# Two four-head softmax attentions: products of keys by queries and of queries by keys issued together, in half steps

## What is computed

```python
def _L3_attn_ref(x, Q, K, VO):
    q = jnp.einsum('btd,hrd->bhtr', x, Q)
    k = jnp.einsum('bud,hrd->bhur', x, K)
    scores = jnp.einsum('bhtr,bhur->bhtu', q, k) / sqrt(d)
    attn = jax.nn.softmax(scores, axis=-1)
    ctx = jnp.einsum('bhtu,bud->bhtd', attn, x)
    return jnp.einsum('bhtd,hde->bte', ctx, VO)

def _L3_ffn_ref(x, ln1_w, ln2_w, wq, wk, wv, wo, router_w, w1, w2, w3):
    h = _rmsnorm(x, ln1_w)
    ...
    scores = jnp.einsum('bhtd,bhsd->bhts', q, k) / jnp.sqrt(jnp.float32(HD))
    scores = jnp.where(causal[None, None], scores, jnp.float32(-1e+30))
    att = jax.nn.softmax(scores, axis=-1)
    y = jnp.einsum('bhts,bhsd->bhtd', att, v).transpose(0, 2, 1, 3).reshape(Bx, Tx, Cx)
    x = x + y @ wo.T
```

## Time and profile before

| | us |
|---|---|
| runs (three) | 1031.77, 1028.7, 1040.98 |
| median | 1031.77 |
| span of the profiled execution | 1033.0 |
| PE busy in it | 920.6 (89%) |
| DVE busy | 645.0 (62%) |
| ACT busy | 367.8 (36%) |
| POOL busy | 226.8 (22%) |

### The profile page before, as it was taken

One profiled execution on the slowest core, in us unless ns is written; L12 is line 12 of the kernel. 1 busy time (PEld: TensorE's weight loads), 2 busy tenths in 40 slices (PEclk: granted clock), 3 DMA queues, 4 the chain that ended last, 5 costly groups with the idle time before them and its releaser, 6 DMA issues. The chain is left out here.

```text
span 1033.0 us, 17166 instructions
## 1 busy us (share of the span) xinstructions
PE 920.6 (89%) x6700; PEld 464.5 (45%) x6700; DVE 645.0 (62%) x1728; ACT 367.8 (36%) x644; POOL 226.8 (22%) x289
## 2 busy tenths in 40 slices
PE   1898788889999888999798899999999899989998
PEld 0588566652323346753474333333333444443333
DVE  4978555667765368985547555455553655577665
ACT  0113532334543343225415324444444032342222
POOL 2700022215335123420330310121223402200000
PEclk9989898999999999999957989999999987999999
DMA  9300300000000001000000000000000000000000
GB/s 309 86 1 2 100 2 1 2 2 1 1 1 1 1 1 43 2 1 1 1 1 2 0 1 1 1 1 2 1 1 1 1 1 1 2 1 1 6 6 11
DMA packets 11476, 15.40 MB, mean 15 GB/s; under 512 B 8268, under 2 KB 9324, under 8 KB 10398
## 3 DMA queue, kind: packets, MB, share of 16 engines
q1 hardware_dynamic: 9976, 13.20, 4.1%
q10 hardware_dynamic: 1418, 1.09, 0.4%
HBM read 13.76 MB, written 0.52 MB: 14 GB/s over the span
## 5 line engine op out<-in xcount | busy, mean ns | idle before, releaser
L633 DVE TENSOR_REDUCE mx<-PS 128x2 f32<-128x1024 f32 (+3 forms) x104 | 109.6, 1096 | 98.0 <-PE PS L440 93.9
L593 ACT ACTIVATE arena<-PS 128x1024 f32<-128x1024 f32 (+3 forms) x104 | 91.0, 924 | 129.8 <-PE PS L470 129.8
L1231 DVE TENSOR_TENSOR arena<-arena,PS 128x512 f32<-128x512 f32 (+1 forms) x144 | 97.1, 685 | 45.2 <-ACT arena L1206 40.5
L1132 PE MATMUL PS<-XT,late 64*128 64x512 f32 (+1 forms) x288 | 101.6, 647 | 4.8 <-DVE L L1874 2.0
L485 PE MATMUL PS<-arena 128*64 128x512 f32 (+3 forms) x416 | 101.4, 578 | 0.5 <-DVE arena L694 0.4
L465 PE MATMUL PS<-arena 32*128 32x512 f32 (+4 forms) x416 | 78.4, 625 | 10.2 <-ACT arena L570 7.4
L1206 ACT ACTIVATE arena<-PS,f_b_sb 128x512 f32<-128x512 f32 x96 | 61.9, 686 | 63.6 <-PE PS L1132 62.2
L1164 PE MATMUL PS<-arena,late 128*64 128x512 f32 (+1 forms) x288 | 81.6, 617 | 1.0 <-DVE arena L1231 0.9
L440 PE MATMUL PS<-arena 32*128 32x512 f32 (+4 forms) x416 | 69.3, 609 | 4.2 <-ACT arena L566 1.6
L1132 PEld LDWEIGHTS PS<-XT,late 64*128 64x128 f32 (+1 forms) x288 | 28.5, 184 | 56.4 <-ACT arena L1206 41.5
L1206 ACT ACTIVATE arena<-PS 114x512 f32<-114x512 f32 x48 | 27.4, 596 | 67.6 <-PE PS L1134 66.9
(11 more groups left out here) (427 smaller groups left out, 1675.2 us busy)
## 6 DMA issues: line engine op xcount, KB each, us to landing
arena<-in_rel SPq DMA_DIRECT2D x4, 1024.0 KB, 12.0
late<-in_edges SPq DMA_DIRECT2D x2, 1024.0 KB, 11.1
late<-in_w_f_w SPq DMA_DIRECT2D x3, 342.0 KB
arena<-in_adj SPq DMA_DIRECT2D x1, 1024.0 KB, 6.8
late<-in_w_f_w SPq DMA_DIRECT2D x2, 512.0 KB, 4.1
Cc<-in_consts SPq DMA_DIRECT2D x1, 916.0 KB
arena<-in_ids ACTq DMA_DIRECT2D x1, 800.0 KB
late<-in_w_f_w SPq DMA_DIRECT2D x4, 128.0 KB, 3.5
```

The costliest lines, as they stand in the source:

```text
L593: nc.scalar.activation(PT[:, s % 2, p, :, queries(c)], PS[:, a:a + 2, queries(c)], ACT.Exp, scale=scale).then_inc(exp_done.sem, 1)
L633: v.reduce_max(mx[:, g % 2, c, 2 * p:2 * p + 2], PS[:, a:a + 2, keys(c)], axis=AX.X).then_inc(max_done.sem, 1)
L1132: ins = nc.tensor.matmul(PS[0:rows, up_bank(n), :], w1(i)[r], XT2[r, b * S:(b + 1) * S], start=True, stop=True)
L1231: nc.vector.tensor_tensor(HG[0:rows, n % 4, :], ha, PS[0:rows, gate_bank(n), :], ALU.mult).then_inc(gated_done.sem, 1)
```

## The change

Nothing of the arithmetic changes, and the count of instructions on each engine is the same. In the two four-head attentions a step becomes two half steps. `opposite(s, p)` issues the column products of pair p of step s, then the row products of the other pair of step s+5, then the subtraction for pair p, then (masked) the masks of the other pair. A step is `opposite(s, 0)`, the turned maxima (c = 3) or the projection (c = 2), `mix(s-1, 0)`, `opposite(s, 1)`, the turned input (c = 0), `mix(s-1, 1)`, the output products (c = 1). The list `units` follows this order, so each unit's bank and the unit that it waits for change too. ACT's and DVE's orders follow: exponential of pair 0, copies of turned maxima or projection, exponential of pair 1; on DVE the maxima of one pair at a time, each in front of the zeroing of the pair of column products issued with it. The two-head attention keeps its order. Functions that nothing called are removed.

```diff
         for s, (g, c) in enumerate(steps):
-            units += [("B", s, p) for p in range(NPAIR)]
+            units += [("B", s, 0)]
+            if s + ahead < U:
+                units += [("A", s + ahead, p) for p in range(1, NPAIR)]
             if s == 0 and weights is not None:
                 units += [("W", 0, 0)]
+            if c == 3 and g + 1 < G and NPAIR == 2:
+                units += [("T", g + 1, 0)]
             if c == 2 and g + 2 < G:
                 units += [("P", g + 2, k) for k in range(PU)]
+            units += [("B", s, p) for p in range(1, NPAIR)]
             if s + ahead < U:
-                units += [("A", s + ahead, p) for p in range(NPAIR)]
+                units += [("A", s + ahead, 0)]
...
+                def opposite(s, p):
+                    r = s + ahead if NPAIR == 2 and s + ahead < U else None
+                    column_products(s, p)
+                    if r is not None:
+                        row_products(r, 1 - p)
+                    less_maxima(s, p)
+                    if causal and r is not None:
+                        row_masks(r, 1 - p)
...
                 for s in range(U + 1):
-                    if s < U:
-                        cols(s)
+                    if s == U:
+                        for p in range(NPAIR):
+                            mix(s - 1, p)
+                        break
+                    g, c = steps[s]
+                    opposite(s, 0)
                     if s == 0 and weights is not None:
                         weight_products()
+                    if c == 3 and g + 1 < G and NPAIR == 2:
+                        maxima(g + 1)
+                    if c == 2 and g + 2 < G:
+                        proj(g + 2)
                     if s >= 1:
                         mix(s - 1, 0)
-                    if s == U:
-                        if NPAIR == 2:
-                            mix(s - 1, 1)
-                        break
-                    g, c = steps[s]
-                    if c == 2 and g + 2 < G:
-                        proj(g + 2)
-                    if s + ahead < U:
+                    if NPAIR == 2:
+                        opposite(s, 1)
+                    elif s + ahead < U:
                         rows(s + ahead)
...
                 for s, (g, c) in enumerate(steps):
-                    if causal:
-                        for p in range(NPAIR):
+                    for p in range(NPAIR):
+                        if NPAIR == 2 and s + ahead < U:
+                            maximum(s + ahead, 1 - p)
+                        if causal:
                             x = PT[:, s % 2, p, :, c * P:(c + 1) * P]
                             eng.wait_ge(exp_done.sem, at(exp_done, s * NPAIR + p))
                             v.scalar_tensor_tensor(out=x, in0=x, scalar=3.0e38, in1=bc(causal[1], 1, 2), op0=ALU.min, op1=ALU.mult).then_inc(later_zeroed.sem, 1)
-                    if rope and c == 2 and g + 2 < G:
-                        turned_pairs(g + 2)
+                        if p == 0 and rope and c == 2 and g + 2 < G:
+                            turned_pairs(g + 2)
```

More of the change, by code:

```diff
@@ L6 @@
-from contextlib import ExitStack, contextmanager, nullcontext
+from contextlib import ExitStack, nullcontext
 import numpy as np
@@ L38, in __init__ @@
         self.count = 0
[L41 to L53, removed]
 def bc(ap, axis, n):
@@ L177, in flat @@
         return t[:].rearrange("p a b -> p (a b)")
[L180 to L199, removed]
@@ L588, in _, with exponentials @@
                     qk(g)
+                def exponentials(s, p):
+                    c = steps[s][1]
+                    a = bank(("B", s, p))
+                    eng.wait_ge(cols_done.sem, at(cols_done, s * NPAIR + p))
+                    nc.scalar.activation(PT[:, s % 2, p, :, queries(c)], PS[:, a:a + 2, queries(c)], ACT.Exp, scale=scale).then_inc(exp_done.sem, 1)
                 for s, (g, c) in enumerate(steps):
-                    for p in range(NPAIR):
-                        a = bank(("B", s, p))
-                        eng.wait_ge(cols_done.sem, at(cols_done, s * NPAIR + p))
-                        nc.scalar.activation(PT[:, s % 2, p, :, queries(c)], PS[:, a:a + 2, queries(c)], ACT.Exp, scale=scale).then_inc(exp_done.sem, 1)
+                    exponentials(s, 0)
                     if s == 0 and weights is not None:
@@ L626, in turned_pairs, with maximum @@
                         v.tensor_tensor(RS[:, k, :], PS[:, a + 1, :], rope[1], ALU.mult).then_inc(roped.sem, 1)
+                def maximum(s, p):
+                    g, c = steps[s]
+                    a = bank(("A", s, p))
+                    eng.wait_ge(rows_done.sem, at(rows_done, row_place(s, p)))
+                    v.reduce_max(mx[:, g % 2, c, 2 * p:2 * p + 2], PS[:, a:a + 2, keys(c)], axis=AX.X).then_inc(max_done.sem, 1)
                 def maxima(s):
                     g, c = steps[s]
-                    for p in range(NPAIR):
-                        a = bank(("A", s, p))
-                        eng.wait_ge(rows_done.sem, at(rows_done, s * NPAIR + p))
-                        v.reduce_max(mx[:, g % 2, c, 2 * p:2 * p + 2], PS[:, a:a + 2, keys(c)], axis=AX.X).then_inc(max_done.sem, 1)
+                    if not swapped(s):
+                        for p in range(NPAIR):
+                            maximum(s, p)
                     if c == TB - 1:
@@ L1034, in linear_attention @@
             signal.count += k
-    def weight_products(pairs, dst, split):
-        with stage(pe=1, act=1) as (block, tallies):
-            @block.tensor
-            def _(eng):
-                pe, _, _, _ = tallies()
-                for n, (l, r) in enumerate(pairs):
-                    ins = nc.tensor.matmul(PS[0:D, 0, n * D:(n + 1) * D], l, r, start=True, stop=True)
-                ins.then_inc(pe.up(), 1)
-            @block.scalar
-            def _(eng):
-                pe, act, _, _ = tallies()
-                eng.wait_ge(tensor_done.sem, pe.at(1))
-                nc.scalar.copy(dst[:, 0:len(pairs) * D], PS[0:D, 0, 0:len(pairs) * D]).then_inc(act.up(), 1)
     pickh = sb("pickh", [P, 16], BF16)
```

195 lines of the change are left out of this document (52 added, 143 removed).

## The result

| | before | after |
|---|---|---|
| runs of both on the same chip (twenty each), median | 1034.65 us | 1047.9 us |
| lowest to highest | 1028.27 to 1041.66 | 1041.24 to 1068.88 |
| ratio, 95% interval | | 1.0117 (1.0083 to 1.015) |
| span of the profiled execution | 1033.0 | 1048.8 |
| mean granted clock in it | 0.938 | 0.929 |

The changed kernel is slower by 1.2%, some 12 us, and the forecast was no change at 1032, with 1022 to 1041 around it.

A forecast was written before the change was run, and what follows sets the result against it. TensorE was taken as the bound in the plain attention, busy 175.8 of 181.2 us. Plain -1.1 and masked +2.5 sum to +1.4 on 1033.0; forecast median 1032, no change, range 1022 to 1041 for 8 times in 10.

The forecast's parts named there:

- -5.3: Plain attention, five middle groups: gain of 1.06 each, from the turned maxima's 0.68 wait and late second pairs.
- -1.5: Plain attention, first group: a gain taken as 1.5 us, between 0 and 4, since waits for the first maxima stay.
- +5.7: Plain attention, last five steps: pairs alone lose 7.1 us, less two late second pairs and one wait of 0.68.
- the rival of 1100: Both attentions: row products don't start beside the other pair's column products, some +70 us, 1100; chance 0.02.
- the faster rival: Exponential frees its bank earlier, all halves 2.28 (3.3 us); masked attention keeps 2.4 GHz (5.8 us); 1023; chance 0.2.
- 2.44: Plain attention: length in us of every other half step, its row products waiting 0.36 for the previous half's exponential.
- No wait, with 0.2 to spare: Plain attention, turned maxima: split ready 3.5 us after the half's start at c = 2, TensorE asks at 3.7.
- The mask portions: Masked attention: masks in two portions cost 0.21 us each, +1.0 over eleven steps, +3.6 at the drain rule's bound.
- The waits at c = 3: Masked attention, two groups: 0.6 for the second rotary product's bank, 1.95 at the turned maxima; 2.6 against 1.8, +1.6.
- if the clock does what it does now: Condition on the masked attention's +2.5 us, the sum of +1.0 masks, +1.6 waits, -2.7 late pairs and +2.6 tail.
- 5.8 for 20.5: Masked attention, price of the clock: 20.5 us at the lower level cost 5.8 us, between 0 and 10.3.
- The slower rival: Masked attention: clock falls more often, 41 us at the lower level costing 5.8 more, tail another 4; 1042; chance 0.2.

The follow-up runs named there:

- filled: Kernel before with half steps in the masked attention alone, plus matmuls nobody reads in its waits at c = 3; ratio 1.0049, median 1038.21 us.
- after, unchanged copy: The changed kernel executed once more with nothing changed, for a second trace of its clock; measured 1059.92 us.

## Why the prediction was wrong, point by point

**The plain attention was right in sum, with two errors in it that offset.** Forecast -1.1, made of -5.3, -1.5 and +5.7; measured at equal clock -2.1, made of -5.7, -2.1 and +5.8. A tail step of lone pairs, forecast at 4.57, in the changed kernel:

```profile
779.44 1.13 PE L336 MATMUL PS<-arena 32*128 32x512 f32 x4
...
784.01 1.13 PE L336 MATMUL PS<-arena 32*128 32x512 f32 x4
```

784.01 - 779.44 = 4.57. Row products do run beside the other pair's column products, which disposes of the rival of 1100. A half step in all engines that matter:

```profile
646.03 0.70 PE L336 MATMUL PS<-arena 32*128 32x512 f32 x2
...
646.07 0.70 PE L304 MATMUL PS<-arena 32*128 32x512 f32 x2
...
647.00 0.38 PE L343 MATMUL PS<-arena,minus 32*128 32x512 bf16 x2
...
647.31 1.08 PE L367 MATMUL PS<-arena 128*64 128x512 f32 x4
647.42 1.02 ACT L477 ACTIVATE arena<-PS 128x1024 f32<-128x1024 f32 x1 [1.18 <-PE PS L343]
...
648.32 0.70 PE L336 MATMUL PS<-arena 32*128 32x512 f32 x2
...
648.49 0.70 PE L304 MATMUL PS<-arena 32*128 32x512 f32 x2
```

Here one term was mis-sized. The exponential starts 647.42 - 646.03 = 1.39 behind its column products, not 1.57 as with four heads, and ends at 648.44. Row products start at 648.49, which is 2.46 after the half's start and 0.17 into the next, where I had 2.64 and 0.36. At 0.17 they end inside the column chain, so all halves are 2.28, as the faster rival had it for this part, and the "2.44" didn't come. That gives back 3 x 0.16 a group, 2.4 in the five middle ones. The other error goes the other way: for the split I had "No wait, with 0.2 to spare". In two of the five middle groups there is one, at 711.87 and 757.19:

```profile
711.87 0.38 PE L326 MATMUL PS<-identh,arena 128*128 128x128 bf16 x4 [0.61 <-DVE arena L553]
```

Together these take 1.2 us. So the nearness of the sum is in part luck.

**The masked attention's work was right too.** Forecast +2.5. At 2.4 GHz throughout the half-step order takes 80.1 (filled); that of before takes 78.1 with 3.4 us at the lower level and 80.0 with 10.2, so an estimated 77.1 with none, by the line through both: +3.0. Of this the tail, forecast at +2.6, is +3.2 (80.1 with lone pairs, 76.9 with joined ones, neither with time at the lower level), and all other terms together are -0.2, forecast at -0.1. The mask portions, forecast at 0.21:

```profile
846.66 0.29 PE L312 MATMUL PS<-causalh,identh 128*128 128x128 bf16 x2
...
846.88 0.87 PE L367 MATMUL PS<-arena 128*64 128x384 f32 x4
```

0.22 to the next row. Two masks take 0.22 and four take 0.33, so some 0.11 of a portion doesn't shrink with the masks. The rule on draining in the Trainium skill (TensorEngine Tiling, Key Properties), weighed in the forecast, can have cost at most that here; at its bound of 0.33 the term would have been +3.6.

The waits at c = 3, for which I had 0.6 and 1.95:

```profile
848.34 0.49 PE L336 MATMUL PS<-arena 32*128 32x128 f32 x4 [0.59 <-DVE arena L524]
...
849.68 0.38 PE L304 MATMUL PS<-arena 32*128 32x128 f32 x2 [0.85 <-POOL arena L632]
...
851.08 0.38 PE L326 MATMUL PS<-identh,arena 128*128 128x128 bf16 x4 [0.69 <-DVE arena L553]
```

Their sum is 2.13 (2.6 forecast), in three portions: row products wait for the keys that POOL finishes, a wait that I hadn't counted apart, and that takes most of what I had put at the turned maxima. At the end of the third group the wait is 1.49, as forecast (1.5):

```profile
904.51 0.38 PE L326 MATMUL PS<-identh,arena 128*128 128x128 bf16 x4 [1.49 <-DVE arena L553]
```

**The step that failed** is the clause behind that sum: "if the clock does what it does now". I gave it 0.55 and its opposite 0.2, while the same text said that idle time at c = 3 grows. Two things were wrong in it. First, "now" was one profile: 20.5 us at the lower level. Later profiles of the same order have 3.4, 10.2 and, with the masked attention left as before in the plain half-step kernel, 10.2 again; the half-step order has 23.9, 27.3 and 62.5. Second, the price. From 0 to 23.9, 27.3 and 62.5 us at the lower level the half-step stretch goes from 80.1 to 90.6, 90.8 and 106.4, about 0.42 us for each us, where I took "5.8 for 20.5", 0.28. For the order of before that was near: its loops of 78.1, 80.0, 80.0 and 83.4 us, with 3.4, 10.2, 10.2 and 20.5, rise by 0.31. The half-step order pays more for the same time at the lower level.

One of my signs of being wrong was a clock of the masked stretch that moves by more than 0.05. The first pair of profiles (0.88 and 0.87) doesn't show it; the later ones lie further apart (0.94 and 0.98 with the old order, 0.85 and 0.71 with half steps).

Together: three profiles of the half-step order have a mean of 96.0 us for the masked loop and four of the old order 80.3, which is more than the 12 us measured over many executions; the longest, 106.4, is from a single long execution, and without it the difference is 10. Of this +3.0 is work and waiting, and the rest is the clock's.

**The slower rival** had the mechanism and came near with its price, 1032 + 10 = 1042; the median of before was 2.9 higher in the larger sample. But its condition was at the wrong place. It was to decide where the idle time at the turned maxima exceeds 1.1. In the first two groups that is 0.69, and still the clock fell: the fall at 852.62 came behind three waits of 0.59, 0.85 and 0.69, which lie between 847.75 and 851.08. In the third group it is 1.49, and there the clock fell in one profile of the half-step order (after, unchanged copy) and not in the other two. Nor does the clock fall much oftener, as the rival had it. In four profiles with the old order in the masked attention it falls at seven of the eight ends of a first or second group, behind waits of 0.48 and 0.64, and stays down for 3.4 to 13.7 us, 6.3 on average; in three with half steps it falls at all six and stays down for 10.2 to 17.1, 13.7 on average. What grew is above all the time that it stays down. Nor is the tail a cause by itself, as I had it: with lone pairs and filled waits it stays at 2.4 GHz; what lone pairs seem to do is keep the clock down once it has fallen at the tail's start (37.5 us, in both profiles where it fell there). In three profiles with joined pairs it fell there too, and was up again after 3.4 us each time. No run isolates this.

Shown by experiment: the loss is in the masked attention alone; over half of it goes when the waits are filled with unread work, and in the masked stretch lone pairs cost 3.2 us beside that. With both mended the whole is under before, though a part of that gain lies outside the stretch. Not shown: how little waiting would do, and why work issued in the same order has 88.7 to 136.5 us at the lower level ahead of the attentions. I didn't try the fillers in the old order.

## What to carry to other kernels

When a change leaves a busy TensorE with more or other short waits, price the clock as a term of its own, from several profiles of the same order, and not as something that stays as it is. Work in which only some of the row groups are busy should be kept short: with both pairs together a step of the plain tail is done in 3.15 instead of 4.57 us. And keep it away from a place where the clock may fall, as far as the few profiles here go. And before a wait is moved, ask what else ends within it: one that is released by the copy may be covering one for the maxima.

## What the runs showed of the hardware that I had not expected

- TensorE stayed at the lower level for 37.5 us while it was busy for 36.99 of them, with lone pairs of 32-row products, output products and mixes (a second profile: 37.15 of 37.50); with both pairs together it was up again after 3.4 us in the same part of the program, in three profiles.
- Short waits between groups of matmuls are enough for the clock to fall. At waits of 0.59, 0.85 and up to 0.69 us, close together, it fell each time, eight times in four profiles, in the second wait at the earliest; at 0.48 and 0.64 in seven places of eight. At a single wait it fell not always: at 1.28 once of two times, at 1.48 to 1.50 three times of five. The Trainium skill (TensorE: Matmul & The Clock Gate, A second HAM failure mode: psum-queue depth-cycling) describes such a kernel, in which short idling between groups of matmuls makes the clock go back and forth; the traces here agree, with 10.24 and 13.65 us at 0.5 behind two such places.
- The kernel before already has matmuls that nobody reads, in other places (eleven in a row from 543.98, L2052). In the waits inside the loop they were worth their time: seven in each of three groups brought the granted clock of the stretch from 0.85 to 1.00 and the stretch from 90.9 to 80.1 us.
